# A second feed-forward that runs inside the last steps of an attention stream instead of in a block of its own

## The reference, cut to what matters

```python
x = x + attention_a(layernorm(x), ...)      # 32 heads of 16, rotary, causal
x = x + ffn(layernorm(x), ...)
x = x + attention_b(layernorm(x), ...)      # 32 query heads of 128, 8 key heads, ALiBi, RMS norms
x = x + ffn(layernorm(x), ...)

def ffn(x, W_base, b_base, W_router, lora_A, lora_B):      # D = O = 512, 8 experts of rank 16
    logits = x @ W_router.T
    topk_p, topk_i = top_k(softmax(logits), 2)
    topk_p = topk_p / sum(topk_p)
    w = sum(one_hot(topk_i, 8) * topk_p[..., None], axis=1)
    h = einsum('td,erd->ter', x, lora_A)
    lora_out = einsum('ter,eor,te->to', h, lora_B, w) * 2.0
    return x @ W_base.T + b_base + lora_out
```

## Time and profile before

| what | value |
|---|---|
| median of 3 runs | 1632.83 us (1631.46 to 1633.01) |
| profiled execution: its time | 1630.95 us |
| profiled execution: its span, first to last instruction | 1629.0 us |
| PE busy in the span | 1517.6 us (93%) |
| DVE busy | 1120.6 us (69%) |
| ACT busy | 814.9 us (50%) |
| POOL busy | 392.6 us (24%) |
| mean granted TensorE clock | 0.981 of full |

### The profile page before, as it was taken

How to read it: one execution, slowest core, us unless ns; L and a number is a source line. 1 busy time by engine, 2 the same in 40 slices (tenths; PEclk the granted TensorE clock), 3 DMA queues, 4 the chain that set the end, 5 groups by cost and what they waited for, 6 DMA issues and landing times. The chain is left out here.

```text
span 1629.0 us, 25348 instructions
## 1 busy us (share of the span) xinstructions
PE 1517.6 (93%) x8968; PEld 1177.1 (72%) x8968; DVE 1120.6 (69%) x2853; ACT 814.9 (50%) x2108; POOL 392.6 (24%) x360
## 2 busy tenths in 40 slices
PE   3998999998997999999999999999999999999969
PEld 2863444443786888888888888888888888888757
DVE  5658777770665676677677677677677767767745
ACT  3523555566323455555555555555556555555521
POOL 4102000011643131431331322233143133131120
PEclk9997999999998999999999999999999999999979
DMA  4363453301101000100100100010010010000011
GB/s 147 97 137 53 54 62 45 40 2 60 59 7 39 1 27 1 39 27 1 40 21 7 40 8 21 1 39 27 1 40 27 1 39 27 1 1 1 1 46 53
DMA packets 40350, 54.53 MB, mean 33 GB/s; under 512 B 5792, under 2 KB 21408, under 8 KB 40224
## 3 DMA queue, kind: packets, MB, share of 16 engines
q1 hardware_dynamic: 40224, 52.91, 13.5%
HBM read 44.31 MB, written 8.39 MB: 32 GB/s over the span
## 5 line engine op out<-in xcount | busy, mean ns | idle before, releaser
L1709 ACT ACTIVATE prob<-prob,ab_neg_max 128x128 f32<-128x128 f32 (+7 forms) x256 | 201.1, 786 | 253.9 <-DVE ab_neg_max L1816 252.9
L1833 DVE TENSOR_TENSOR ab_pt_l<-ps,ab_pt_h 128x512 fp32r<-128x512 f32 x288 | 198.0, 688 | 73.8 <-ACT ab_pt_h L1737 72.9
L1737 ACT CAST ab_pt_h<-ps 128x512 fp32r<-128x512 f32 x288 | 171.6, 598 | 109.3 <-PE ps L1622 108.7
L1816 DVE CUSTOM_DVE_ANT_0 prob<-ps,rel 128x512 f32<-128x512 f32 (+3 forms) x256 | 146.0, 570 | 100.9 <-PE ps L52 100.0
L50 PE MATMUL ps<-ab_w_h,ab_xt_h 128*128 128x512 f32 (+1 forms) x512 | 186.2, 364 | 6.7 <-DVE ab_v_l L1853 6.0
L1040 DVE TENSOR_REDUCE ra_part_max<-ps 128x1 f32<-128x512 f32 (+3 forms) x318 | 156.5, 552 | 47.8 <-PE ps L942 28.7
L1622 PE MATMUL ps<-ident,prob 128*128 128x128 f32 x1152 | 173.5, 273 | 5.8 <-DVE ab_qt_l L1825 4.5
L1841 DVE TENSOR_SCALAR prob<-prob,ab_recip 128x128 f32<-128x128 f32 (+7 forms) x256 | 168.5, 658 | 9.1
L52 PE MATMUL ps<-ab_w_h,ab_xt_l 128*128 128x512 f32 (+1 forms) x512 | 174.1, 340 | 0.0
L51 PE MATMUL ps<-ab_w_l,ab_xt_h 128*128 128x512 f32 (+1 forms) x512 | 173.4, 339 | 0.0
L1622 PEld LDWEIGHTS ps<-ident,prob 128*128 128x128 f32 x1152 | 138.0, 140 | 26.6 <-DVE ab_qt_l L1825 5.8
(11 more groups left out here) (257 smaller groups left out, 3468.0 us busy)
## 6 DMA issues: line engine op xcount, KB each, us to landing
f_raw<-in_wqkv SPq DMA_DIRECT2D x32, 384.0 KB, 3.6
f_raw<-in_wbo SPq DMA_DIRECT2D x32, 256.0 KB, 2.6
ra_first_rows<-parts SPq DMA_DIRECT2D x36, 128.0 KB, 6.7
parts<-pa_stage SPq DMA_DIRECT2D x12, 256.0 KB, 3.1
parts<-f_raw SPq DMA_DIRECT2D x12, 256.0 KB, 3.3
ra_q_st<-parts SPq DMA_DIRECT2D x24, 128.0 KB, 6.5
ra_k_st<-parts SPq DMA_DIRECT2D x24, 128.0 KB, 7.0
f_raw<-in_wf SPq DMA_DIRECT2D x8, 324.0 KB, 4.0
```

The lines of the kernel that those rows point to most:

```text
L1709: act.activation(prob[:, t % 2, h, 0:w], prob[:, t % 2, h, 0:w], ACT.Exp, bias=neg_max[:, t % 2, h, pieces_per_head(t % NT) - 1:pieces_per ...
L1737: act.copy(pt_h[:, n % PT, :], ring_bank("p", u, j)).then_inc(pt_high, 1)
L1816: dve.tensor_tensor_reduce(out=prob[:, t % 2, h, k0:k1], in0=ps[:, n % 2, a:b], in1=const["rel"][:, SLIDE - i * P + k0:SLIDE - i * P + k1] ...
L1833: dve.tensor_tensor(pt_l[:, n % PT, :], ring_bank("p", u, j), pt_h[:, n % PT, :].bitcast(F32), ALU.subtract).then_inc(emptied, 1)
```

## The change

The block `ffn_block` and its helpers are gone. The second feed-forward becomes tiles 8 to 15 of the same two objects, `f_norm` and `ff`, that make the first, and runs in `stream_block` from step 61 on.

A stream step now also has two halves of four quarters: slots 0 to 3 and 4 to 7 (`half_of`). From half 0 (slots 4 to 7 of step 61) each half starts a tile of the second feed-forward by the list `SECOND_TILES`: tiles 0 to 5 in halves 0 to 5, tile 6 in half 7, tile 7 in half 9. A tile takes three halves: in the first its moments, inversion and centring; in the second its turning, `hidden`, ranking, division and routing; in the third `turn_weighted`, `main`, `finish` and `add`. Halves 1 to 8 lie in steps 62 to 65; halves 9, 10 and 11 follow the stream. In each slot an engine first does what the stream gives it and then its part `second(half, q)`.

The weights of the feed-forward are loaded by SP behind the last weights of the attention, split by ACT and POOL in slots 0 to 3 of step 60 and slot 0 of step 61, and lie in columns of `xt_h` and `xt_l` (and rows of `v_h`, `v_l`) that are no longer read. Turning and `hidden` of the second feed-forward use bank 2, `main` and `finish` use bank 3, both free after the last projection; the routed values are turned in the ring of banks 4 to 6, as jobs "w" that `shared_jobs` plans. `route` and the bias (`offset`) are POOL's in it, where `ffn_block` had them on DVE. The stores are issued by SP at the end of `stream_block`, tile by tile as they are added.

The core of the diff:

```diff
+SECOND = B_STEPS - 3
+SECOND_TILES = (0, 1, 2, 3, 4, 5, None, 6, None, 7)
+SECOND_HALVES = len(SECOND_TILES) + 2
+
+def second_tiles(half, *lags):
+    at = [SECOND_TILES[half - lag] if 0 <= half - lag < len(SECOND_TILES) else None for lag in lags]
+    return [i if i is None else NT + i for i in at]
+
+def half_of(t, s):
+    return 2 * (t - SECOND) - 1 + s // 4, s % 4
+
+def weighted_quarter(i):
+    return 1 if i < 2 * NT - 1 else 2
...
         def _(sp):
...
+            for k in range(KC):
+                load(S_PIECES + k, ins["wf"][k * P:(k + 1) * P, :])
+            load(S_PIECES + KC, ins["wb"])
+            for i in range(NT):
+                sp.wait_ge(ff.added, NT + i + 1)
+                sp.dma_start(out_dram[i * P:(i + 1) * P, :], x[:, i, :]).then_inc(out_stored, 16)
+            sp.wait_ge(out_stored, 16 * NT)
...
         def _(pool):
+            def second(half, q):
+                v, a = second_tiles(half, 0, 1)
+                if q == 0 and a is not None:
+                    ff.offset(pool, a)
+                if q == 3 and v is not None:
+                    f_norm.invert(pool, v)
+                if q == 3 and a is not None:
+                    ff.route(pool, a)
...
+                    if t == SECOND - 1 and s < KC:
+                        split_low(S_PIECES + s)
+                    if t == SECOND and s == 0:
+                        split_low(S_PIECES + KC)
+                    second(*half_of(t, s))
...
         def _(pe):
+            def second(half, q):
+                a, b = second_tiles(half, 1, 2)
+                if q == 0 and a is not None:
+                    if a == NT:
+                        pe.wait_ge(scaled, B_STEPS)
+                    else:
+                        pe.wait_ge(ff.hid_out, a)
+                    f_norm.turn(pe, a)
+                if q == 1 and b is not None:
+                    if q == weighted_quarter(b):
+                        ring_free("w", b)
+                        ff.turn_weighted(pe, b)
+                    ff.main(pe, b)
+                if q == 2 and b is not None:
+                    if q == weighted_quarter(b):
+                        ring_free("w", b)
+                        ff.turn_weighted(pe, b)
+                    ff.finish(pe, b, (emptied, job_of["w", b][0] + 1))
+                if q == 2 and a is not None:
+                    ff.hidden(pe, a)
...
         def _(act):
+            def second(half, q):
+                a, b = second_tiles(half, 1, 2)
+                if q == 1 and a is not None:
+                    if a >= NT + 2:
+                        act.wait_ge(ff.summed, a - 1)
+                    f_norm.high(act, a)
+                if b is not None and q == weighted_quarter(b):
+                    ff.high_weighted(act, b)
+                if q == 2 and a is not None:
+                    ff.take_hidden(act, a)
+                if q == 3 and a is not None:
+                    ff.weigh(act, a)
...
         def _(dve):
+            def second(half, q):
+                v, a, b = second_tiles(half, 0, 1, 2)
+                if q == 1 and a is not None:
+                    f_norm.low(dve, a)
+                if b is not None and q == weighted_quarter(b):
+                    ff.low_weighted(dve, b, emptied)
+                if q == 2 and v is not None:
+                    dve.wait_ge(emptied, job_of["o", B_STEPS - 2 * NT + v][0] + 1)
+                    f_norm.moments(dve, v)
+                if q == 3 and a is not None:
+                    ff.rank(dve, a)
+                if q == 3 and v is not None:
+                    f_norm.centre(dve, v)
+                if q == 3 and a is not None:
+                    ff.divide(dve, a)
+                if q == 3 and b is not None:
+                    ff.add(dve, b)
...
+            for half in range(2 * (B_STEPS + 2 - SECOND) - 1, SECOND_HALVES):
+                for q in range(4):
+                    second(half, q)
...
-        with ExitStack() as own:
-            ffn(own, "f2")(out_dram)
```

More of the change, by code:

```diff
@@ L383, in high_weighted, with low_weighted, finish @@
             act.wait_ge(self.summed, i)
-        act.copy(self.ht_h[:, :], self.hw_bank[:, 0:P]).then_inc(self.ht_high, 1)
-    def low_weighted(self, dve, i):
+        act.copy(self.ht_h[:, :], self.hw_bank(i)[:, 0:P]).then_inc(self.ht_high, 1)
+    def low_weighted(self, dve, i, done=None):
         dve.wait_ge(self.ht_high, i + 1)
[L388 to L395, removed]
+        dve.tensor_tensor(self.ht_l[:, :], self.hw_bank(i)[:, 0:P], self.ht_h[:, :].bitcast(F32),
+                          ALU.subtract).then_inc(self.ht_low if done is None else done, 1)
+    def finish(self, pe, i, ready=None):
+        pe.wait_ge(*((self.ht_low, i + 1) if ready is None else ready))
+        if i % NT == 0:
+            pe.wait_ge(*self.weights_in(i, KC))
+        three_pass(pe, self.main_bank(i), (self.ht_h[:, :], self.ht_l[:, :]), self.wb(i),
                    False, True).then_inc(self.summed, 1)
@@ L1695, in _, with split_high_of @@
                     step(m - LEAD)
+            for half in range(2 * (B_STEPS + 2 - SECOND) - 1, SECOND_HALVES):
+                for q in range(4):
+                    second(half, q)
         @block.scalar
         def _(act):
[L1699 to L1704 removed]
+            def split_high_of(n):
+                columns, high, _ = raw_of(n)
+                act.wait_ge(raw_in[n % KC], 16 * (n // KC + 1))
+                act.copy(high, raw[:, n % KC, 0:columns]).then_inc(split_high, 1)
+            def second(half, q):
[10 more added lines that the diff above has]
+                    ff.weigh(act, a)
             def exponent(t, h):
```

311 lines of the change are left out of this document (79 added, 232 removed).

## The result

The changed kernel took 1618.46 us (median of four runs, 1617.08 to 1619.58) beside 1632.92 us (1631.46 to 1633.58) for the kernel before, run next to it: a ratio of 0.9914 with a 95% interval from 0.9902 to 0.9925, or 14.5 us less. The profiled execution took 1617.08 us with a span of 1615.3 us. A single execution in all that follows, 1727.18 us at a mean clock of 0.843 in the experiment with the short bias, ran slow throughout and is left out of its median.

The account below looks back on a forecast made before the run. PE, busy 93% of the span, was taken as the bound, so gains lie in its idle or slow time. Mix at 1591.1, project_out's end 1597.3, span's end 1613.5: 15.5 us less, 1632.8 to 1617.3 us; range 1612.2 to 1627.

Parts of the forecast that it names:

- splits: Step 60: four casts on ACT and four subtractions on POOL for the second weights cost 1.0 us, bounds 0 and 2.95.
- stream gaps covered: Stream gaps of 1.17 us (low part of queries) and 1.01 us (shifted scores) get covered by hidden or main: -2.2 us.
- mix to project_out's end: Step 65 behind tile 63's last mix: hidden of tile 6 fills the 2.69 us gap except 1.6 us; 6.2 us in all.
- stage: Length from the add that ends step 59 to the span's end; predicted terms sum to 136.4 us.
- insertion: Before tile 63's last mix PE also gets turn, hidden, main and finish of tiles 0 to 5: 32.6 us.
- waits before the mix: New PE waits: 1.5 us before main in the middle of step 64, 1.0 us for small waits in all other halves.
- Two signs: Profile after, if right: PE busy above 95% in steps 62 to 64; waits for centred tiles at L240 would mean wrong.
- tail: From project_out's end to the span's end, with the last tile's chain in it: 16.2 us.
- Halves as chains: Rival: PE stalls for scores in each half, deciding from 2.6 us a half; at full chain 1636 us; chance 0.09.
- The clock in the tail: Rival: a tail gap lowers PE's clock, hidden and main of tile 7 take longer: +4.1 us, 1621.4 us; chance 0.14.
- DVE as the bound: Rival: in steps 62 and 63 POOL holds up each of DVE's eight normalisings: about +6 us, 1623.3; chance 0.13.
- Everything hides: Rival: no split cost, no routing wait, and step 65's gap filled, giving 1612.2 us; chance 0.12.

Follow-up runs that it names:

- the experiment with the short bias: Changed kernel with POOL adding the second feed-forward's bias to 8 columns instead of 512, the rest left out; 1619.37 us, ratio 0.9923 to the kernel before.
- e7_small_split: Changed kernel with POOL's subtraction for the second weights over 8 columns instead of 648 or 512, other low parts stale; 1618.35 us, ratio 0.9918.
- e3_behind: Changed kernel with all eight tiles of the second feed-forward run behind the stream; 1659.26 us, ratio 1.0168 to the kernel before.
- the last experiment: Changed kernel with norm, ranking through routing, and ACT's high copy each earlier, plus tile 5 one half later; 1615.26 us, ratio 0.9907.
- e8_early_high: Changed kernel with only ACT's high copy of the turned tile moved from quarter 1 to quarter 0; 1618.78 us, ratio 0.9927.
- e4_weighted_late: Changed kernel with turn_weighted a quarter later, behind main instead of in front of it; 1633.06 us, ratio 1.0008 to the kernel before.

## Why the prediction was right

The time predicted was 1617.3 us, 1.2 us under the measured median and inside the range. The terms, each counted from the add that ends step 59:

| term | predicted us | measured us | read from |
|---|---|---|---|
| that add to the last mix's end | 114.0 (1591.1 - 1477.11) | 116.4 (1592.50 - 1476.12) | timeline |
| of it waits of PE in front of woven pieces | 2.5 | 5.1 | five rows above |
| splits | 1.0 | 1.3 | step 60: 16.92 against 15.62; of it POOL's subtractions 0.7 (e7_small_split) |
| stream gaps covered | 2.2 | both gone | waits after |
| mix to project_out's end | 6.2 | 6.6 | last matmul 1598.73 + 0.40 |
| project_out's end to span's end | 16.2 | 16.2 | 16.14 from the add |
| stage | 136.4 | 139.2 | sum |

**The insertion** held: 32.6 us of PE for six tiles at full clock. From the two lengths to the mix, 80.1 us before (1557.21 - 1477.11) and 116.4 after, the difference is 36.3 us; less 5.1 of waits, 1.3 of splits, and with the two gaps of 2.2 us given back, it leaves 32.1. The splits were 0.3 us under-priced and the insertion 0.5 over-priced, which nearly cancel.

**The waits before the mix** are the term that was too small, by 2.6 us; the stage came out 2.8 us longer. I counted the waits for centred tiles "at nothing because centring is ready a slot and more before". That is wrong: they were 3.0 us, because the centring stands behind the ranking's first part and two stream operations in DVE's order. The wait I did name, 1.5 us in front of the weighted turn in the middle of step 64, was 0.40 us, since the turn two pieces ahead of it had already waited 1.14. With the centring early it came out at 1.43 us. The 1.68 us of the first hidden, behind ACT's exponential, was in no term of its own; 1.0 us for all small waits had to hold it. Two signs that the prediction had set were therefore missed: the busy share above 95% in steps 62 to 64 (87% and 94% in two of them), and no waits for centred tiles.

**The 1.2 us at the median** is less than the 2.8 us of the stage because the profiled execution had gained 1.0 us ahead of the change and because medians and single spans differ by some tenths. That part was luck: by the stage alone, 12.7 us less, the time would have been 1620.1 us.

**The tail** was right as a whole, and in its parts: the last tile's hidden starts after a wait of 1.53 us (predicted 1.4), turn_weighted and finish wait 0.47 and 0.68 us, and the closing add starts at 1612.15, 3.15 us before the end (predicted 3.1).

The rivals. **Halves as chains**: its threshold was 2.6 us of stall a half; the seven halves before the mix had 0.7 us on average. Without the stream beside them the same halves do run as chains, 4.9 us a half over PE's need with the slower clock in it, and the kernel is slower than before. Its mechanism is real and the cover decides. **The clock in the tail**: gaps of 1.53 us at 1594.62 and at 1605.26, and the matmuls behind them took 0.28 us (256 wide) and 0.40 us (512 wide) each; the granted clock of the stretch was 0.98, so 2.4 GHz. It did not occur. **DVE as the bound**: the lock was seen, as the Trainium skill ("SBUF — State Buffer", section "Who interferes with whom") has it, with 1.73 us against 0.76: the normalising was 0.97 us longer, where POOL's bias still had 1.18 us to run when it started. The rival had let all eight normalisings of a step be held up; the bias met two of the eight, and taking the bias away changed nothing. **Everything hides**: no, 5.1 us did not. Moving the links of the chain earlier within a half brings that down to 1.2 us.

Step 61 came out 0.7 us longer by its adds (17.48 us against the 16.74 of the earlier trace rows), but PE did not lose that time. From the add that starts it to the start of project_out's last matmul are 16.3 us in both kernels (1509.05 - 1492.73 and 1509.35 - 1493.04). In the changed kernel the first tile's moments and its centring stand in front of the add in DVE's order:

```profile
1510.06 0.55 DVE L233 TENSOR_SCALAR ab_xn<-x,f1n_mean_var,f1n_rstd 128x512 f32<-128x512 f32 x1 [0.19 <-POOL f1n_rstd L225]
1510.52 0.68 DVE L1867 TENSOR_TENSOR x<-ps,x 128x512 f32<-128x512 f32 x1
```

With all halves behind the stream (e3_behind) step 61 took 16.75 us. An add to x is a good mark only where nothing new stands in front of it.

Open: why executions differ ahead of the stage. For the larger part they do so before the first add of the middle steps, which started between 410.98 and 413.53 us in the fourteen profiled executions.

## What to carry to other kernels

Work woven tile by tile into a busy stream costs the bound engine its own time plus the links of the tile's chain that come too late. List for each woven piece the operations queued in front of its producer on that producer's engine, not only the length of the chain: here the in-order queue of DVE made a centring late that had been reckoned ready. When one wait in a chain is removed, look for the next link before counting the gain: the 3.0 us of waits for centred tiles, removed alone, gained 0.4 us; all links and the earlier copy together gained 4.6 us. Measure such small edits from a mark inside the kernel just ahead of the change, where the length of the one repeated kernel came out the same within 0.02 us, since here the whole time varies by 2 us and more for other reasons.

## What the runs showed of the hardware

Once PE's clock followed, a late value cost more than the wait. Slower matmuls added 4.7 us to 9.5 us of idle with turn_weighted late, 7.2 us to 12.6 with the routed values in bank 2, and 18.4 us to 23.0 with the feed-forward behind the stream.

Behind single gaps of up to 2.04 us (the last experiment) matmuls 512 wide stayed at 0.40 us, and behind one of 2.18 us (e8_early_high) four turns took 0.63 us and the next matmuls 512 wide 0.39. Behind gaps of 2.35, 2.73, 3.28 and 4.10 us matmuls 512 wide took 0.63 us. This lies on both sides of what the earlier trace rows show, 1.66 us harmless and 2.37 us not.

But the length of the gap does not decide alone. Behind one of 2.10 us near the end of e3_behind the first matmul 512 wide took 0.50 us, the next four 0.39 to 0.40, and from 1649.22 us on six took 0.63:

```profile
1647.65 0.50 PE L50 MATMUL ps<-ab_xt_h 128*128 128x512 f32 x1 [2.10 <-DVE x L408]
...
1649.65 0.63 PE L51 MATMUL ps<-ab_xt_l,ab_xt_h 128*128 128x512 f32 x1
```

The gap of 2.69 us behind the last mix is the same in the kernel before and in e3_behind. In the first the slow matmuls began 1.3 us behind its end (0.56 us at 1561.16, then 0.63), in the second at once. So the runs give no one length that parts harmless gaps from costly ones, 2.10 us having cost where 2.18 did not, and the drop can come some matmuls later than the gap.

Two smaller gaps can do it as well. With the feed-forward behind the stream the two gaps of 1.38 and 1.55 us have only the four turns (0.63 us) between them, and the matmuls behind the second one took 0.63 us:

```profile
1608.04 0.74 PE L50 MATMUL ps<-ab_xt_h 128*128 128x512 f32 x1
1608.58 0.63 PE L51 MATMUL ps<-ab_xt_l,ab_xt_h 128*128 128x512 f32 x1
```

The same pair of gaps, 1.36 and 1.52 us, had the same effect at the end of e4_weighted_late (matmuls 256 wide at 0.42 us instead of 0.28). In the changed kernel the gaps of 1.4 to 1.7 us (at 1515.49, 1521.40, 1594.62 and 1605.26) each stand alone between longer runs of matmuls, and the matmuls behind all of them kept to 0.28 us (256 wide) and 0.40 us (512 wide).
